# One core, attention and feed-forward with decay scans: loops written out, small vector steps merged or moved to ScalarE and TensorE

## The reference

```python
def bi_wkv(r, k, v, w, u, time_emb):          # k = v = fside
    tf = sigmoid(sum(time_emb, -1))
    decay = exp(-exp(w)) * (0.5 + 0.5 * tf)
    ek = exp(minimum(k, 30)); ekv = ek * v
    nf, df = scan of  a = a * decay + ekv,  b = b * decay + ek   # over the positions
    nb, db = the same, from the last position to the first
    euk = exp(minimum(u + k, 30))
    num = nf + nb - ekv + euk * v
    den = df + db - ek + euk
    return sigmoid(r) * num / maximum(den, 1e-8) * (0.8 + 0.2 * tf)

x = x + attention(bi_wkv(x, fside, fside, w1, u1, cond), w_qkv, w_o)   # 16 heads of 32, causal softmax
h = bi_wkv(x, fside, fside, w2, u2, cond)
inter = silu(q_act(h) @ q_w(w_gate).T) * (q_act(h) @ q_w(w_up).T)      # 512 -> 2048
x = x + q_act(inter) @ q_w(w_down).T                                   # 2048 -> 512
```

## Time and profile before

| what | value |
|---|---|
| runs | 1191.45, 1195.66, 1196.83 us; median 1195.66 |
| profiled execution: span from first to last instruction | 1187.8 us |
| the profiled execution's own time | not given by the page; the span is 7.9 us below the median of the runs |
| busy: PE / DVE / ACT | 789.4 (66%) / 924.9 (78%) / 354.8 us (30%) |
| mean granted clock of TensorE | 0.856 of full speed |

### The profile page before, as it was taken

How to read it: one execution, slowest core, us unless ns; L and a number is a source line. 1 busy time by engine, 2 the same in 40 slices (tenths; PEclk the granted TensorE clock), 3 DMA queues, 4 the chain that set the end, 5 groups by cost and what they waited for, 6 DMA issues and landing times.

```text
span 1187.8 us, 12534 instructions
## 1 busy us (share of the span) xinstructions
PE 789.4 (66%) x3648; PEld 385.7 (32%) x3648; DVE 924.9 (78%) x1576; ACT 354.8 (30%) x648; POOL 2.8 (0%) x15
## 2 busy tenths in 40 slices
PE   0000018167878997578779986687789966887585
PEld 0000003033443443344434432333444423454232
DVE  6999999768787588877892897788856987862587
ACT  3101001034455230244552221345452303444030
POOL 0000000000000000000000000000000000000000
PEclk9999999577768999678678997777699997799798
DMA  8312120333400000732200004434000034330001
GB/s 337 123 44 75 40 79 0 70 81 89 116 18 19 0 1 23 201 80 78 57 18 10 1 1 123 115 76 125 10 19 1 1 101 121 80 71 1 1 1 36
DMA packets 34429, 72.51 MB, mean 61 GB/s; under 512 B 5808, under 2 KB 5808, under 8 KB 32560
## 3 DMA queue, kind: packets, MB, share of 16 engines
q1 hardware_dynamic: 30032, 63.73, 19.6%
q10 hardware_dynamic: 4320, 7.87, 2.2%
HBM read 33.82 MB, written 4.19 MB: 32 GB/s over the span
## 4 chain that ended last, share of the span: by engine, by line
DVE 40%; PE 34%; issue 17%; ACT 4%; DVEq 2%; DMA 1%; SPq 1%; ACTq 0%
PE bank L813 8%; PE bank L888 5%; PE bank L906 4%; PE bank L804 4%; PE bank L846 3%; PE bank L825 3%; DVE negmax L682 3%; DVE region L779 2%; PE bank L859 2%; DVE region L523 2%; PE bank L847 2%; DVE attn L502 2%; ACT region L382 2%; DVE ekv L580 2%; DVE region L471 2%
## 5 line engine op out<-in xcount | busy, mean ns | idle before, releaser
L825 PE MATMUL bank<-stacks 128*128 128x128 f32 (+3 forms) x256 | 125.4, 499 | 110.6 <-DVE negmax L682 76.0
L682 DVE TENSOR_REDUCE negmax<-bank 128x1 f32<-128x128 f32 (+3 forms) x256 | 117.7, 484 | 88.6 <-PE bank L827 87.2
L804 PE MATMUL bank<-wqkv,h 128*128 128x512 f32 x128 | 59.5, 621 | 173.2 <-DVE h L633 173.2
L846 PE MATMUL bank<-stacks 128*128 128x512 f32 (+3 forms) x256 | 124.9, 488 | 41.5 <-ACT region L382 41.1
L813 PE MATMUL bank<-h,wqkv 128*128 128x512 f32 x256 | 134.4, 680 | 5.1 <-DVE region L779 5.1
L382 ACT ACTIVATE region<-bank 128x512 f32<-128x512 f32 (+3 forms) x256 | 103.9, 432 | 108.9 <-PE bank L848 106.9
L825 PEld LDWEIGHTS bank<-stacks 128*128 128x128 f32 x256 | 61.7, 241 | 141.6 <-DVE negmax L682 89.6
L847 PE MATMUL bank<-maxrow,pick 128*128 128x512 bf16 (+3 forms) x256 | 94.5, 369 | 0.0
L804 PEld LDWEIGHTS bank<-wqkv,h 128*128 128x128 f32 x128 | 25.1, 199 | 204.4 <-issue 204.4
L326 ACT ACTIVATE fd<-fd,omd 128x512 f32<-128x512 f32 x32 | 23.0, 720 | 223.8 <-DVE ends L585 223.8
L846 PEld LDWEIGHTS bank<-stacks 128*128 128x128 f32 x256 | 61.8, 242 | 61.9 <-ACT region L382 53.5
(11 more groups left out here) (113 smaller groups left out, 1298.4 us busy)
## 6 DMA issues: line engine op xcount, KB each, us to landing
stacks<-halves SPq DMA_DIRECT2D x256, 128.0 KB, 3.2
kt<-in_fside ACTq DMA_DIRECT2D x30, 256.0 KB, 3.1
h<-in_x SPq DMA_DIRECT2D x4, 1024.0 KB, 5.8
region<-in_w_gate SPq DMA_DIRECT2D x4, 1024.0 KB, 11.7
xt<-in_x SPq DMA_DIRECT2D x4, 1024.0 KB, 6.4
region<-in_w_up SPq DMA_DIRECT2D x4, 1024.0 KB, 5.6
region<-in_w_down SPq DMA_DIRECT2D x4, 1024.0 KB, 4.8
out<-xt SPq DMA_DIRECT2D x16, 256.0 KB, 2.9
```

The source lines that it names most:

```text
L682: nc.vector.tensor_reduce(negmax[:, g % 2, t, i:i + 1], bank[2 + n % 2][:, 0:P * (t + 1)], AX_X, ALU.max, negate=True).then_inc(max_taken, 1)
L804: mm = nc.tensor.matmul(bank[4 + t % 2][:, :], h[:, j, P * t:P * t + P], wqkv[:, j, 2 * C:3 * C], start=(j == 0), stop=(j == CJ - 1))
L825: nc.tensor.matmul(o[:, 0:P * (t + 1)], qs[s][:, i, P * t:P * t + P], ks[s][:, i, 0:P * (t + 1)], start=True, stop=False)
L846: nc.tensor.matmul(o, ks[s][:, i, P * t:P * t + P], qs[s][:, i, P * t:T], start=True, stop=False)
```

## The change

It is in twelve parts.

1. `Fori` goes; the four turns are written out, so the constants of each batch are read from tables made at setup (`omd2_all`, `half_ln_gain`, `two_root_gain`) and `batch_constants` goes.
2. `weigh` leaves the last position as it is, and the backward scan starts from 0: the two `ends` go.
3. The floor goes from `add_own`. ACT's reciprocal becomes Relu(den - floor), Ln(+ floor), Exp, with half the logarithm of the gain as bias; `finish` takes the maximum within its first product.
4. `low_parts` goes from DVE. TensorE subtracts the high half in the bank itself (`leave_low`, a product with minus the identity), and ACT copies what is left.
5. `leave_low` of group 1 stands behind score steps 4 and 5; of groups 2 and 3 behind steps 10 and 11 of groups 0 and 1; of the next batch's group 0 behind its projection, ahead of the gate products.
6. ACT's `low_parts` stands: for group 1 behind `reciprocals(b, 0)`; for groups 2 and 3 between exponentials 9 and the reciprocals ahead of exponential 10.
7. DVE splits the maxima before the transposes (`split_maxima`, in the place of `max_low`), TensorE turns both halves with bf16 products, and ACT stores them in one copy (`copy_maxima`).
8. Gate and up are made two blocks at a time, in 2 sets of 4 banks; silu and the multiply take 1024 columns.
9. ACT takes the magnitudes of a pair into `size` (`sizes`), which has one buffer: the next pair waits for `raise_top` of the one before.
10. DVE keeps the elementwise maximum of the upper 16 bits of `size` in `top2` (`raise_top`) and cuts to the exponent once, at the end.
11. `cap` waits for its own earlier scans.
12. `stack(0, 0)` no longer has a DVE step of its own ahead of it.

```diff
             def weigh(b, u):
...
-                    nc.scalar.activation(tile[:, :], tile[:, :], ACT.Copy,
-                                         scale=omd2[:, CJ * second + j:CJ * second + j + 1]).then_inc(weighted, 1)
+                    nc.scalar.activation(tile[:, 0:T - 1], tile[:, 0:T - 1], ACT.Copy,
+                                         scale=omd2_all[:, b + 1 - second, CJ * second + j:CJ * second + j + 1]).then_inc(weighted, 1)
             def reciprocals(b, u, last=2 * CJ):
-                act.wait_ge(den_ready, U + 1)
-                nc.scalar.activation(rec[:, :], den[:, :], ACT.Ln).then_inc(rec_ready, 1)
-                act.wait_ge(rec_ready, 2 * U + 1)
-                nc.scalar.activation(rec[:, :], rec[:, :], ACT.Exp, scale=-1.0).then_inc(rec_ready, 1)
+                act.wait_ge(summed, U + 1)
+                nc.scalar.activation(rec[:, :], den[:, :], ACT.Relu, bias=-DEN_FLOOR).then_inc(rec_ready, 1)
+                act.wait_ge(rec_ready, 3 * U + 1)
+                nc.scalar.activation(rec[:, :], rec[:, :], ACT.Ln, bias=DEN_FLOOR).then_inc(rec_ready, 1)
+                act.wait_ge(rec_ready, 3 * U + 2)
+                nc.scalar.activation(rec[:, :], rec[:, :], ACT.Exp, scale=-1.0,
+                                     bias=half_ln_gain[:, b + 1 - second:b + 2 - second]).then_inc(rec_ready, 1)
+            def low_parts(b, g):
+                qk_bank = qk_banks(g)
+                for s in range(2):
+                    act.wait_ge(qk_rest, b * (2 * GROUPS) + 2 * g + s + 1)
+                    nc.scalar.activation(halves[:, 2 * s + 1, :], qk_bank[s][:, :], ACT.Copy).then_inc(qk_low, 1)
+            def sizes(b, f):
+                n = b * (FJ // 2) + f
+                act.wait_ge(inter_ready, n + 1)
+                if f:
+                    act.wait_ge(tops, n)
+                else:
+                    act.wait_ge(xq_ready, b + 1)
+                nc.scalar.activation(size, inter[:, 2 * f:2 * f + 2, :], ACT.Abs).then_inc(abs_ready, 1)
...
                     exps(b, g, 6, 10)
+                    if g < 2:
+                        low_parts(b, g + 2)
                     if u < scans:
                         reciprocals(b, u, last)
                     exps(b, g, 10, 12)
...
-            with act.Fori(0, B - 1) as b:
-                turn(b, True)
-            table(6)
-            turn(B - 1, False)
+            for b in range(B):
+                turn(b, b + 1 < B)
...
-                nc.vector.tensor_tensor(ends[:, 0:1], fd[:, T - 1:T], d, ALU.mult).then_inc(fwd_ready, 1)
-                nc.vector.tensor_tensor(ends[:, 1:2], fn[:, T - 1:T], d, ALU.mult).then_inc(fwd_ready, 1)
...
-                nc.vector.tensor_scalar(den[:, :], den[:, :], DEN_FLOOR, None, ALU.max).then_inc(den_ready, 1)
...
-                nc.vector.tensor_tensor(den[:, :], den[:, :], rec[:, :], ALU.mult).then_inc(newton, 1)
+                nc.vector.scalar_tensor_tensor(den[:, :], den[:, :], DEN_FLOOR, rec[:, :], ALU.max, ALU.mult).then_inc(newton, 1)
...
-            def max_low(b, g):
-                dve.wait_ge(mt_high, b * GROUPS + g + 1)
-                nc.vector.tensor_tensor(maxrow[HD:HD + HG, g % 2, :], bank[2][0:HG, :], maxrow[0:HG, g % 2, :],
-                                        ALU.subtract).then_inc(mt_low, 1)
+            def split_maxima(b, g):
+                n = b * GROUPS + g
+                dve.wait_ge(max_taken, (n + 1) * UNITS)
+                nc.vector.tensor_copy(negmax_hl[:, g % 2, :, 0, :], negmax[:, g % 2, :, :]).then_inc(max_split, 1)
+                dve.wait_ge(max_split, 2 * n + 1)
+                nc.vector.tensor_tensor(negmax_hl[:, g % 2, :, 1, :], negmax[:, g % 2, :, :], negmax_hl[:, g % 2, :, 0, :],
+                                        ALU.subtract).then_inc(max_split, 1)
+            def raise_top(b, f):
+                n = b * (FJ // 2) + f
+                dve.wait_ge(abs_ready, n + 1)
+                if f:
+                    dve.wait_ge(tops, n)
+                    nc.vector.tensor_tensor(top2, top2, size_high, ALU.max).then_inc(tops, 1)
+                else:
+                    nc.vector.tensor_copy(top2, size_high).then_inc(tops, 1)
...
                 finish(b, 0)
-                max_low(b, 0)
+                split_maxima(b, 0)
...
                         backward(b, u + 1)
                     if g + 1 < GROUPS:
-                        max_low(b, g + 1)
+                        split_maxima(b, g + 1)
...
-                for f in range(FJ):
-                    dve.wait_ge(silu_ready, b * FJ + f + 1)
-                    nc.vector.tensor_tensor(inter[:, f, :], bank[2 * (f % 4) + 1][:, :], silu[:, f % 2, :],
-                                            ALU.mult).then_inc(inter_ready, 1)
-                    dve.wait_ge(inter_ready, b * FJ + f + 1)
-                    magnitude(qc, inter[:, f, :], f == 0)
+                for f in range(FJ // 2):
+                    n = b * (FJ // 2) + f + 1
+                    at = 4 * (f % 2) + 2
+                    dve.wait_ge(silu_ready, n)
+                    dve.wait_ge(up_ready, n)
+                    nc.vector.tensor_tensor(inter[:, 2 * f:2 * f + 2, :], banks[:, at:at + 2, :], silu[:, f % 2, :, :],
+                                            ALU.mult).then_inc(inter_ready, 1)
+                    if f:
+                        raise_top(b, f - 1)
+                raise_top(b, FJ // 2 - 1)
+                dve.wait_ge(tops, (b + 1) * (FJ // 2))
+                qc.link(nc.vector.tensor_tensor(top_e, top2[:, 0, :], top2[:, 1, :], ALU.max))
+                qc.link(nc.vector.tensor_scalar(top_e.bitcast(U16), top_e.bitcast(U16), 0x7F80, None, ALU.bitwise_and))
...
+            def leave_low(b, g, s):
+                pe.wait_ge(qk_high, b * (2 * GROUPS) + 2 * g + s + 1)
+                nc.tensor.matmul(qk_banks(g)[s][:, :], less_ident[:, :], halves[:, 2 * s, :],
+                                 start=False, stop=True, skip_group_check=True).then_inc(qk_rest, 1)
...
             def transpose_maxima(b, g):
-                pe.wait_ge(max_taken, b * (GROUPS * UNITS) + (g + 1) * UNITS)
+                pe.wait_ge(max_split, 2 * (b * GROUPS + g + 1))
                 for t in range(TT):
-                    mm = nc.tensor.transpose(bank[2][0:HG, P * t:P * t + P], negmax[:, g % 2, t, :], ident[:, :])
+                    mm = nc.tensor.matmul(bank[2][0:2 * HG, P * t:P * t + P],
+                                          negmax_hl[:, g % 2, t, :, :].rearrange("p c i -> p (c i)"), identb[:, :],
+                                          start=(t == 0), stop=(t == TT - 1), skip_group_check=True)
...
                         if g < 2 and n in (10, 11):
                             leave_low(b, g + 2, n - 10)
```

207 lines of the change are left out of this document (108 added, 99 removed).

## The result

| | median (range), us | ratio to before, 95% interval |
|---|---|---|
| before | 1193.56 (1187.93 to 1196.83, 4 runs) | |
| after | 1206.11 (1204.91 to 1207.12, 4 runs) | 1.0102 [1.0059, 1.0145] |

The change makes the kernel 1.0% slower: 12.5 us, where 24.8 were forecast. 1206.1 lies inside the range and 14.4 under the predicted time. In the runs of the experiments, two executions (1384 us of one kernel, 1360 of the kernel before) were far slower than all others at a lower granted clock, and are left out of the ratios.

What follows compares the result with a forecast made beforehand. By busy shares DVE bounds the kernel, but in attention it and TensorE hand work to each other and neither is full. The terms summed to +24.8 us on 1195.7, giving 1220.5 us, range 1176 to 1236.

Steps and rivals of the forecast that it cites:

- The start: Setup to the first score: DVE spared work and batch 0's stacking no longer behind low halves and clamps, -5.8 us.
- the wait ahead of the gate products: Before gate/up: second subtraction product waits for ScalarE's high copy and delays the first gate product, +1.15 us, three times.
- the tail: Last up product to first shuffle: pair's multiply, maxima and magnitudes take 5.6 us instead of 2.6, +3.0 four times.
- the handovers to groups 1 and 2: Between last and next first maximum: to group 1 -3.0 us in sum, to group 2 +5.7 by the load of `kt`.
- The first rival: DVE's saving arrives at steps 10 to 12 of groups 0 and 1 and the handovers: 1163 us, chance 0.17.
- the term inside group 1: Step 12 waits behind ScalarE's low copies: +0.7 us in each of three batches, +3.1 in batch 3, +5.2 in sum.
- colder TensorE: Rival: longer gaps before transposes and at step 12 hold attention at 1.2 GHz, +4 a batch: 1236 us, chance 0.13.
- The term of `kt`: Handover from group 1 to 2: later row copy and relu delay the load of `kt`, +1.9 us, +5.7 in sum.
- the handover to group 3: From group 2 to 3, TensorE being last: +0.4 us a batch, +1.2 in sum.
- The turns and first groups: To group 1's first maximum: loops written out -2.9 us, first groups with transposes behind the split +3.6; +0.7 in sum.
- Inside group 0: Step 12 waits for an exponential behind ScalarE's low copies; scans cover 2.2 of 3.4 us: +1.2, +4.8 in sum.
- Group 3: To the output projection's first product: relu ahead of the exponentials at a lower clock, +0.65 us, +2.0 in sum.

Runs made afterwards that it cites:

- experiment 3: The changed kernel with ScalarE's low parts for groups 2 and 3 moved behind the exponentials of steps 10 and 11; 1191.36 us, ratio 0.9984.
- experiment 2: The changed kernel with the split of the maxima ahead of the first finish and the backward scans; 1197.15 us, ratio 1.0032.
- experiments 4 and 5: Changed kernel with a pair's magnitudes and maximum ahead of the next's silu and multiply, 1200.98 us; with second subtraction product behind first gate products, 1204.31 us.
- experiment 8: The kernel before with eight needless TensorE products per batch in the pause ahead of group 1's query projection; 1187.22 us, ratio 0.9954.
- two edits of order: Split of the maxima first and ScalarE's low parts later, added to the changed kernel with single gate and up blocks; 1165.54 us, ratio 0.9761.
- the kernel with single blocks: The changed kernel with gate and up made block by block and the magnitudes DVE's again; 1195.1 us, ratio 1.0004.
- the best kernel: The changed kernel with single blocks, split first and low parts later: 1165.54 us; with eight needless products per batch added: 1161.39 us, ratio 0.9731.
- experiment 7: The changed kernel with edits 2 to 5 together (split first, low parts later, tops first, subtraction inside) and the last pair's exponents on DVE; 1173.85 us, ratio 0.9833.

## Why the prediction was right in direction and wrong in size

**Right, by mechanism and size.** The start (-5.8, measured -6.0), the wait ahead of the gate products (+1.15 each, 1.2), the tail (+3.0 each, 3.1, with the slow maximum), DVE's 70 us, and that nearly none of it arrives; the handovers to groups 1 and 2 (-3.0 and +5.7, measured -2.0 and +5.3). The first rival, that DVE's saving arrives, fell at step 12: the subtraction products end at 523.5 and 524.4 there, in a group that began 2.2 later than before, and not before 520.0.

**Wrong: the term inside group 1, +5.2.** -3.7 was measured: for the first three batches +0.7 each was forecast, and -3.3, -3.4 and -1.4 came. Its mechanism was there: experiment 3 takes 8.6 us out of this stretch, and its 3.6 in the last batch are close to the forecast 3.1. What failed is the silent assumption that TensorE's products keep the durations of before. The earlier trace rows gave a clock of 0.70 for the whole stage, and I read no clock of a shorter stretch. Behind a pause of 3.30 us, made by TensorE running ahead of DVE, the projection of group 3 ran at 1.2 GHz; the split behind the backward scans, which delays the transposes, took the pause away, and with the split first (experiment 2) it is back in the second and third batch (4.32 us; 1.4 in the first). "TensorE is ready 10.15 after the last maximum and DVE after 9.9" says it already: nobody waits at this place any more. The rival "colder TensorE" had the right cause with the wrong sign.

**The term of `kt`** came as forecast. Counted from the end of the last maximum, in the second batch, ScalarE's row copy is 2.0 us later (2.05 forecast), the load 2.5 (2.7), the finish on DVE 1.9 (1.85), and DVE's next maximum 1.2, in the two other batches 2.0: between 1.1 and 2.7, as the prediction had it. DVE no longer waits for `kt`, which has landed, but for the reciprocals. The maxima of before, then the changed kernel:

```profile
569.27 0.69 DVE L682 TENSOR_REDUCE negmax<-bank 128x1 f32<-128x512 f32 x1 [0.56 <-PE bank L827]
...
582.32 0.61 DVE L682 TENSOR_REDUCE negmax<-bank 128x1 f32<-128x128 f32 x2
```

```profile
569.04 0.69 DVE L701 TENSOR_REDUCE negmax<-bank 128x1 f32<-128x512 f32 x1 [0.20 <-PE bank L862]
...
572.93 0.59 ACT L400 ACTIVATE maxrow<-bank 8x512 bf16<-8x512 f32 x1 [3.79 <-PE bank L868]
...
579.38 0.33 ACTq L349 DMA_DIRECT2D kt<-in_fside  x1
580.13 0.69 DVE L649 SCALAR_TENSOR_TENSOR den<-den,rec 128x512 f32<-128x512 f32 x1 [3.02 <-ACT rec L346]
...
583.26 0.62 DVE L701 TENSOR_REDUCE negmax<-bank 128x1 f32<-128x128 f32 x2
```

**Wrong the other way: the handover to group 3**, +1.2 forecast, +7.4 measured. TensorE is last there, as the prediction says, and the split stands behind the backward scans there too; but I charged it 0.4 a batch, and experiment 2 takes 7.0 out. The turns and first groups, +0.7, took 5.0; with the split first, -1.8. There too its place cost more than the forecast's 1.8 a batch (8.3 in sum), and less was won ahead of the last maximum. Inside group 0, +4.8 was too much: +2.6.

**Luck.** The eight rows of attention miss by some 32 us if each miss is counted without its sign, and by 8.7 in sum. That the total came out within the range owes much to misses that cancelled.

**Open.** Group 3 came out 5.1 us shorter (+2.0 forecast). Nearly all of it is the second batch, where the kernel before took 29.9 us and in the first and third 25.0 and 25.3. The clock of its steps there was 0.94 instead of 0.61:

```profile
612.60:628.90 16.30, 12.91 (x52) 7.04 (x48) 14.03 (x22) 10.94 (x24) 0.00 (x0) 0.61 0.09 33
```

```profile
614.40:627.00 12.60, 8.71 (x49) 5.03 (x49) 9.94 (x15) 9.13 (x22) 0.00 (x0) 0.94 0.06 21
```

But in experiments 4 and 5, which touch nothing there, the same sum was -9.3 and -7.9, and with the products of experiment 8, which lie in group 1, +0.5. The value products of this group alone took 4.5 us at a clock of 1.00 in some batches and up to 7.0 at 0.64 in others, in the kernel before too (6.7 in its second batch). Which part of the change moved it isn't shown.

**The base.** Differences of spans were added to the median. The profiled execution of before was some 4 us under that median and the one of after 1 us over its own, so that +17.5 in the spans is +12.5 in the medians. That makes 5 of the 12.3 us by which the forecast of the difference was too large; the rows of attention make the rest (+15.1 forecast, +6.4 measured), less the 1.5 in the products and some tenths. The other 2.1 of the 14.4 us are the base itself: 1195.66 was the median of three runs, 1193.56 that of four.

## What to carry to other kernels

When two engines hand work to each other, what an edit saves on one counts only up to the other's next wait; order can be worth more than work: two edits of order took 29.6 us off the kernel with single blocks (1195.1 to 1165.5), and undoing the pairs 11.1 off the changed one. A step given to another engine goes behind what that engine's waiters need next, and a step that the next engine needs goes ahead of the scans. Before adding durations of TensorE, read its granted clock for each short stretch, and ask whether the edit makes or removes a pause ahead of it. Compare a forecast with the traces at the points that it was made for: on another engine's points the same handover looked like a miss.

## What the runs showed of the hardware

Eight needless products of TensorE (1.9 us of them in each batch, in a pause of 3.3) made the kernel of before 0.46% faster: the granted clock in that stretch was 0.88 instead of 0.77. Such a gain needn't reach the end: in the best kernel the same products gained 2.8 to 2.9 us a batch in that stretch, and value products later on took 7.0 instead of 4.5 us. A longer wait of TensorE at one place (3.31 instead of 0.79 us ahead of the transposes) went with a higher clock at the next. An elementwise maximum of bf16 with one strided input took 1.22 us for 1024 columns on VectorE, one of packed inputs 0.69 (experiment 7). Relu and Ln on ScalarE took 0.63 each for 512 columns, and Exp 0.63 without a bias tile and 0.72 with one.
